# Edge records scattered one per batch in the second convolution and three per batch in the mean stage, where it was two and two

## The reference

```python
x = _layernorm(x + _L0_gnn_ref(x, edge_index, W1, b1, W2, b2))          # two GCN convolutions
x = _layernorm(x + _L1_gnn_ref(x, edge_index, edge_type_8, W, root, bias))  # 8 relations, mean per relation
x = _layernorm(x + _L2_gnn_ref(x, W2, edge_index, edge_type_8))         # attention over edges of a type
x = _layernorm(x + _L3_gnn_ref(x, W3, edge_index, edge_type_16))        # 16 relations, sum, relu

# one GCN convolution
h = x @ W
msgs = h[src] * (dinv[src] * dinv[dst])[:, None]
out = jax.ops.segment_sum(msgs, dst, num_segments=n_nodes) + b
# the mean layer, for each relation r
msg = (x @ W[r])[src] * mask[:, None]
out = out + segment_sum(msg, dst) / jnp.maximum(deg, 1.0)[:, None]
```

## Time and profile before

| | |
|---|---|
| median of 3 runs | 3365.49 us (3362.89 to 3366.80) |
| profiled execution | 3362.33 us, its span 3360.6 us |
| busy share of the span: PE, DVE, ACT, POOL | 72%, 72%, 51%, 61% |
| second convolution, first to last gather on POOL | 950.1 to 1322.7 us |
| mean stage, first to last gather on POOL | 1370.5 to 1785.2 us |
| gathers and records of the two stages on POOL | 392 and 196 instructions |

### The profile page before, as it was taken

The page is one execution under the profiler, slowest core; times in us unless marked ns, Lnnn a source line. Parts: engine busy times, 40 slices in busy tenths (PEclk is TensorE's granted clock), DMA queues, the critical chain, the costliest instruction groups (busy, mean ns, idle before and its releaser), DMA issues. The chain is left out here.

```text
span 3360.6 us, 55128 instructions
## 1 busy us (share of the span) xinstructions
PE 2418.6 (72%) x9989; PEld 1527.0 (45%) x9990; DVE 2425.5 (72%) x7443; ACT 1711.3 (51%) x4719; POOL 2033.8 (61%) x1982
## 2 busy tenths in 40 slices
PE   2764665677745666699996766676344899999996
PEld 1443443566645556344443333566233444444443
DVE  7998664777858888599995111333777788888886
ACT  1774775788947777466664444454476111111111
POOL 2777774776557775577774775776000466666664
PEclk9997887899968888799998898555555999999998
DMA  2664554445535555355554777898344111111110
GB/s 56 216 213 150 174 176 136 147 154 160 173 114 182 182 188 174 109 155 152 150 155 132 259 265 231 268 289 274 96 153 134 54 43 48 49 47 51 53 52 30
DMA packets 316459, 490.91 MB, mean 146 GB/s; under 512 B 63594, under 2 KB 143497, under 8 KB 316378
## 3 DMA queue, kind: packets, MB, share of 16 engines
q1 hardware_dynamic: 250266, 377.40, 34.6%
q0 software_dynamic: 66112, 112.69, 12.7%
HBM read 260.66 MB, written 233.07 MB: 147 GB/s over the span
## 5 line engine op out<-in xcount | busy, mean ns | idle before, releaser
L1290 PE MATMUL bank<-sum_masked,sum_w 128*128 128x512 f32 x1568 | 691.3, 594 | 1.4 <-DVE sum_masked L1380 1.4
L1163 POOL DMA_INDIRECT sum_rows<-t_x,m_row_int x196 | 223.9, 1142 | 477.8 <-POOLq L118 263.7
L1380 DVE SCALAR_TENSOR_TENSOR sum_masked<-sum_typ,sum_col 128x512 f32<-128x512 bf16 x784 | 489.2, 684 | 19.5 <-ACT sum_col L1218 17.2
L1290 PEld LDWEIGHTS bank<-sum_masked,sum_w 128*128 128x128 f32 x1568 | 291.4, 191 | 332.3 <-issue 272.3
L1290 PE MATMUL bank<-mean_masked,mean_w 128*128 128x512 f32 x784 | 378.2, 613 | 18.2 <-DVE mean_masked L1380 18.2
L1218 ACT ACTIVATE sum_col<-bank 128x512 f32<-128x512 f32 x49 | 29.3, 597 | 578.9 <-PE bank L1336 565.4
L1163 POOL DMA_INDIRECT mean_rows<-t_x,m_row_int x196 | 219.2, 1118 | 103.7 <-issue 59.4
L1180 POOL DMA_INDIRECT out_dram<-sum_new,m_last_int x196 | 219.2, 1118 | 87.2 <-issue 58.2
L1163 POOL DMA_INDIRECT c_rows<-x_dram,m_src_int x196 | 190.3, 971 | 123.0 <-issue 54.6
L1380 DVE SCALAR_TENSOR_TENSOR mean_masked<-mean_typ,mean_col 128x512 f32<-128x512 bf16 x392 | 249.7, 679 | 20.7 <-ACT mean_col L1218 20.5
L1592 POOL DMA_INDIRECT at_xs<-t_x,at_order x204 | 192.9, 946 | 94.4 <-issue 61.0
(11 more groups left out here) (322 smaller groups left out, 5871.3 us busy)
## 6 DMA issues: line engine op xcount, KB each, us to landing
t_hu<-at_made SPq DMA_DIRECT2D x51, 512.0 KB, 3.9
pf_xc<-x_dram SPq DMA_DIRECT2D x98, 256.0 KB, 3.1
t_g<-pf_g SPq DMA_DIRECT2D x98, 256.0 KB
t_x<-pf_x SPq DMA_DIRECT2D x98, 256.0 KB
c_dense_x<-t_x SPq DMA_DIRECT2D x98, 256.0 KB
t_x<-c_dense_x SPq DMA_DIRECT2D x98, 256.0 KB, 3.6
c_same<-p_same SPq DMA_DIRECT2D x98, 128.0 KB, 3.3
t_g<-c_new SPq DMA_DIRECT2D x49, 256.0 KB
```

Of the source, the lines that this page charges most:

```text
L1163: pool.indirect_dma_start(rows[:, s % 2, j, :], None, source, bass.IndirectOffsetOnAxis(ap=index[:, k:k + 1], axis=0))\
L1290: pe.matmul(H[q][:, :], w[:, r, :], masked[:, r % MASKS, :], start=(r == 0), stop=(r == n_rel - 1))\
L1380: v.scalar_tensor_tensor(out=masked[:, r % MASKS, :], in0=typ[:, q, :], scalar=float(r), in1=col[:, q, :], op0=ALU.is_equal, op1=ALU.mult) ...
```

## The change

The number of records per batch becomes one in the second convolution (tiles 0 to 48) and three in the mean stage (tiles 49 to 195). The total stays 196. The gathers, their waits and all other engines are as before.

```diff
-        first_recorded = {CONV2: 0, MEAN: KT // 2}.get(kind)
+        first_recorded, records = {CONV2: (0, 1), MEAN: (NB, 3)}.get(kind, (None, 0))
         recorded = sem.of_pool("recorded")[0] if first_recorded is not None else None
...
                     if recorded is not None:
-                        for j in range(2):
-                            k = first_recorded + s * 2 + j
+                        for j in range(records):
+                            k = first_recorded + s * records + j
                             pool.indirect_dma_start(m.order8, bass.IndirectOffsetOnAxis(ap=m.order_int[:, k:k + 1], axis=0),
                                                     m.row_int[:, k:k + 1], None, bounds_check=P * TA - 1, oob_is_err=False)\
                                 .then_inc(recorded, 16)
...
             if recorded is not None:
-                hold(pool, recorded, KT // 2 * 16)
+                hold(pool, recorded, NB * records * 16)
```

## The result

The changed kernel takes 3430.91 us (median of 4 runs, 3423.82 to 3433.15), the kernel before 3364.19 us with one more run. The ratio is 1.0196, 95% interval 1.0177 to 1.0215: slower by about 66.7 us. The prediction was 3415 us, range 3386 to 3431: the measured median lies 0.1 us inside the upper end. The profiled execution took 3430.38 us, its span 3428.6 us, 68.0 us longer than before.

A forecast was written before the change was run, and what follows sets the result against it. DVE's chain paces the second convolution; POOL, already full, would bound the mean stage. -5.3 us (second convolution's start) + 57.8 us (mean stage) = +52.5 us on 3362.3 gives 3414.8, stated as 3415 us, range 3386 to 3431.

The forecast's parts named there:

- the forecast's own band: The main case: mean-stage period of 9.4 to 10.1 us, total 3396 to 3430 us, given 73%.
- What bounds each stage: DVE's chain with ACT and PE paces the second convolution's steady part; all engines fall to POOL's pace in the mean stage.
- The start of the second convolution: Rows of the first batches come earlier and DVE waits less: -5.3 us, bounds -2.6 and -6.5.
- The third record: Mean stage: a seventh DMA per batch, nothing covering it, lengthens the period from 8.56 to 9.8 us; +58.8 us.
- The low bound: Mean-stage period with seven unstretched DMAs: 7.68 + 1.30 = 8.98 us.
- The stretch: Mean-stage DMAs held up by masked copies: 0.88 us a batch before, 0.90 expected after, then period shaded to 9.8 us.
- the high bound: Mean-stage period with seven DMAs at the stage's present mean of 1.423 us each: 9.96 us.
- The lag of the last batch: Mean stage: last scan's 24.4 us distance from the last batch's first gather shrinks by 1 us, bounds 0 and -4.
- The clock rival: TensorE's granted clock falls in the mean stage; at 0.78 the period is 10.5 us, total 3448 us; 6%.
- the sign that the prediction named for being wrong: One of three such signs: PE's clock drops in the mean stage; no size given.
- The even trade: Rival: POOL paces both stages, so the second convolution gives back up to 62 us; net -9 us, 3353 us; 3%.
- the low stretch: Rival: mean-stage DMAs fall between masks, period 9.0 to 9.4 us; 3387 us at 9.2; 16%.

The follow-up runs named there:

- zero_four: Against the changed kernel: no record per batch in the second convolution, four in the mean stage; 3491.31 us.
- conv_one_alone: Also the alone-run; against the changed kernel: mean stage back at two records per batch, second convolution at one, tiles 49 to 97 left out; 3355.83 us.
- three_one: Against the changed kernel: three records per batch in the second convolution, one in the mean stage; 3411.83 us.
- psum_masks_three: Against the changed kernel: the mean stage's masked copies read their data from PSUM instead of ScalarE's SBUF copy; 3375.07 us.

## Why the prediction was right

The mechanism was forecast: which engine bounds each stage, and that the loss outweighs the gain. That the time lies inside the range at all is luck: it is 0.1 us under the upper end, and the forecast's own band (a period up to 10.1 us, up to 3430 us) was passed on both counts. One term, the period of the mean stage, was too small.

**What bounds each stage: right.** The second convolution was paced by DVE's chain (7.89 us before, 7.93 after, and no closer with no record at all: zero_four has its scans of batches 5 and 45 at 998.77 and 1315.09, 7.91 us a batch, and its stage shortened by 8.7 us, not by the 98 x 1.3 = 127 us that POOL was spared). The mean stage fell to POOL's pace, with ACT waiting for rows in every batch.

**The start of the second convolution: right.** -5.3 us was predicted; -6.2 came by batch 5, inside the bounds of -2.6 and -6.5, and the steady part, priced at 0, gave 1.6 back, so that -4.5 were left at the last scan and -4.3 at the next stage. The alone-run gave -6.0 at its last scan. The 2.72 us wait shrank to 0.45, it didn't vanish.

**The third record: right in kind, too small.** The term that was mis-sized is the period: "I take 8.98 + 0.90 = 9.88 and shade it to 9.8 us" measured 10.11. Over 47 batches the 0.3 us are 15 us, nearly the whole distance from 3415 to 3431. The low bound was exact (8.96 without the stretch). The stretch was not 0.82 but 1.15 us. I had argued that it would thin out, as eight masks spread over a longer batch, and had shaded it down once more. It didn't thin out from six DMAs to seven: it grew from 0.88 to 1.15 us a batch, and even the high bound, seven at the stage's present mean, 9.96, was short of 10.11. What the argument left out is that the alignment itself changes. Before, the same two DMAs of six were hit in 96% of the batches; afterwards the batches vary from 8.94 to 10.87 us as the DMAs slide against the masks. Why they fall as they do on average isn't shown; one schedule gave 10.01 and 10.11 in two kernels.

**The lag of the last batch:** predicted -1, measured (1873.9 - (1855.4 - 3.9)) - 24.4 = -2.0 us.

**The clock rival** did not decide, though the sign that the prediction named for being wrong, a drop of PE's clock in the mean stage, did come in a small way: 0.97 granted, PE 86% busy. PE was not the bound at that clock: POOL waited for another engine for 1.2 of 300 us. Even zero_four, with 0.92 granted from 1400 to 1700 us and PE busy for 236.8 of them, kept to POOL's pace.

**The even trade** was refuted by three_one and conv_one_alone, **the low stretch** by 10.11 us.

## What to carry to other kernels

A queue that is full yet never waits and an arithmetic stage of the same length can sit side by side; moving work into such a stage costs its full price, while the stage that it came from gives back only what its start waited for. Price an added DMA at the mean that DMAs have in the stage where it goes, not where it came from, and give that price a range on both sides, since one more DMA shifts all the others against the instructions that hold them up: here the mean was 1.43 us, the seventh cost 1.55 and the eighth 1.31 to 1.41. Look for idle time of the issuing engine at the start and end of stages, and count how much fits: 20 and 15 records in the tails gained, 26 and 24 gave it back.

## What the runs showed of the hardware

- A masked copy (two SBUF inputs) holds up an indirect DMA that begins on POOL while it runs, by nearly the rest of the mask. In the mean stage of the kernel before, 44 DMAs began with 0.60 to 0.70 us of a mask still to run and took 0.49 to 0.56 us longer than their floor (0.944 us for a gather, 0.994 for a record); 62 began with 0.30 to 0.40 us to run and took 0.20 to 0.28 us longer.
- It can even hold up a DMA that began before it: the record at 1615.08 us took 1.52 us with the mask starting at 1615.09. The timeline of the changed kernel has 17 DMAs of the mean stage that began 11 to 15 ns ahead of a mask, each 1.50 to 1.52 us long; the six that began 27 to 29 ns ahead took 0.99 us, and their masks about 0.70. By the rule of the Trainium skill (page "SBUF — State Buffer", section "Who interferes with whom"), that the one that starts first keeps the ports, the 17 should not have been held and the six masks should have waited for a whole DMA; neither fits. When within its time a DMA reads SBUF isn't shown by any run here.
- The hold is close to one-sided: in psum_masks_three, free of it, a mask of the mean stage has a median of 678 ns and at most 690; with it, in the kernel before, 683 and at most 694. In the changed kernel the median is 684, and the longest is 742, so a mask may lose up to some 60 ns, where a DMA loses over 500:

```profile
L1380 DVE SCALAR_TENSOR_TENSOR mean_masked<-mean_typ,mean_col x392: 656/684/742, 1377.6 to 1871.7; 128x512 f32<-128x512 bf16 x196
```

- Taking one SBUF input away cost the mask nothing and gave 55 us in the changed kernel.
